# Reading the doubt flag two search parts later on VectorE, in a nearest-neighbour attention kernel

## The reference: what is computed

```python
x = x + _L0_conv_ref(_gn(x), L0_conv_weight, L0_conv_bias)   # 3x3, a weight of its own at each of 3136 points
x = x + _L1_conv_ref(_gn(x), ...)                            # neighbour attention
```

```python
p = p / jnp.maximum(jnp.linalg.norm(p, axis=1, keepdims=True), 1e-12)
dist = _pairwise_distance(p)              # 3136 x 3136 for each image
_, nn_idx = jax.lax.top_k(-dist, K)       # the 16 nearest points of each point
nbr = pts[bidx, nn_idx]
logits = leaky_relu(cat([e, e_n]) @ W_att + b_att, 0.1)
attn = softmax(logits, axis=2)
agg = jnp.sum(nbr * attn, axis=2)
y = cat([pts, agg]) @ W_conv + b_conv     # then batch norm, relu, and + pts
```

## Time and profile before

| | |
|---|---|
| median of three runs | 12411.11 us |
| the profiled execution | 12415.89 us, of which the span from first to last instruction is 12414.2 us |
| mean granted TensorE clock | 0.948 of full speed |
| VectorE busy | 10343.8 us (83% of the span) |
| TensorE busy | 10245.6 us (83%) |
| ScalarE busy | 10206.3 us (82%) |
| GpSimd busy | 3005.3 us (24%) |
| `attend` | from about 1519 us to 12310 us |

### The profile page before, as it was taken

The page is one execution under the profiler, slowest core; times in us unless marked ns, Lnnn a source line. Parts: engine busy times, 40 slices in busy tenths (PEclk is TensorE's granted clock), DMA queues, the critical chain, the costliest instruction groups (busy, mean ns, idle before and its releaser), DMA issues. The chain is left out here.

```text
span 12414.2 us, 345180 instructions
## 1 busy us (share of the span) xinstructions
PE 10245.6 (83%) x125146; PEld 7668.4 (62%) x125146; DVE 10343.8 (83%) x23897; ACT 10206.3 (82%) x11576; POOL 3005.3 (24%) x1648
## 2 busy tenths in 40 slices
PE   2774678888888888888888888888888888878875
PEld 2564356666666666666666666666666666656654
DVE  1000599999999999999999999999999999999997
ACT  2332489999898999989999998898998989979986
POOL 0000022222222222222222222222222222222221
PEclk9897889999999999999999999999999999999998
DMA  9666800000000000000000000000000000000003
GB/s 153 169 167 175 254 9 16 17 16 16 16 16 16 16 16 16 5 16 16 16 17 16 17 16 16 16 17 16 17 16 4 16 16 17 16 15 16 16 4 127
DMA packets 267617, 481.85 MB, mean 39 GB/s; under 512 B 196964, under 2 KB 197348, under 8 KB 248356
## 3 DMA queue, kind: packets, MB, share of 16 engines
q1 hardware_dynamic: 261348, 407.82, 13.9%
q0 software_dynamic: 4608, 51.38, 1.2%
HBM read 353.59 MB, written 105.50 MB: 37 GB/s over the span
## 5 line engine op out<-in xcount | busy, mean ns | idle before, releaser
L871 PE MATMUL psum<-ident_a,masked 128*128 128x128 f32 (+1 forms) x40000 | 5529.8, 286 | 575.0 <-ACT turned_sb L991 485.1
L871 PEld LDWEIGHTS psum<-ident_a,masked 128*128 128x128 f32 (+1 forms) x40000 | 4790.7, 193 | 1807.9 <-issue 1733.2
L820 POOL TENSOR_TENSOR masked<-masked,shares_a 128x784 f32<-128x784 f32 x1600 | 2984.7, 1865 | 7765.8 <-DVE doubts L1068 5058.4
L1062 DVE MAX8 found<-scores 128x8 f32<-128x224 f32 x11200 | 3440.0, 378 | 138.6 <-ACT scores L964 63.8
L991 ACT ACTIVATE turned_sb<-psum 128x512 f32<-128x512 f32 (+1 forms) x5600 | 2948.5, 565 | 251.4 <-PE psum L871 177.3
L964 ACT ACTIVATE scores<-psum 128x1568 f32<-128x1568 f32 x1600 | 2372.8, 1483 | 825.4 <-DVE minus_top L1101 712.8
L1101 DVE CUSTOM_DVE_ANT_0 masked<-masked,scores 128x3136 f32<-128x3136 f32 x800 | 2724.3, 3405 | 0.2 <-DVE scores L1093 0.2
L976 ACT ACTIVATE masked<-masked,minus_top 128x3136 f32<-128x3136 f32 x800 | 2353.9, 2942 | 0.0
L956 ACT ACTIVATE masked<-shares_a,own 128x3136 f32<-128x3136 f32 x800 | 2328.2, 2910 | 1.0
L848 PE MATMUL psum<-points 32*128 32x392 f32 x12800 | 1596.0, 564 | 29.8 <-DMA rows<-table 16.9
L890 PE MATMUL psum<-turned_sb,rows 128*32 128x128 f32 (+1 forms) x40000 | 1524.8, 281 | 0.5 <-ACT inverse_sb L972 0.5
(11 more groups left out here) (134 smaller groups left out, 5368.6 us busy)
## 6 DMA issues: line engine op xcount, KB each, us to landing
w_in<-in_L_conv_weight_dram SPq DMA_DIRECT2D x784, 144.0 KB, 2.8
points<-unit SPq DMA_DIRECT2D x128, 392.0 KB
shares_a<-share SPq DMA_DIRECT2D x32, 1568.0 KB
windows<-xg SPq DMA_DIRECT2D x42, 928.0 KB, 11.5
xg<-padded SPq DMA_DIRECT2D x32, 406.0 KB, 17.1
table<-table_sb SPq DMA_DIRECT2D x32, 404.2 KB
rows<-table SPq DMA_DIRECT2D x32, 396.0 KB
x_in<-in_x_dram POOLq DMA_DIRECT2D x8, 1568.0 KB, 12.6
```

The costliest lines, as they stand in the source:

```text
L820: nc.gpsimd.tensor_tensor(m, m, shares[:, t.half, k * width:(k + 1) * width], ALU.add).then_inc(logits_ready, 1)
L871: last = nc.tensor.matmul(ps[0:width, bank + u * P:bank + (u + 1) * P], masked[:, t.ring, j * P:j * P + width], ident[:], start=True, stop ...
L1062: n = step(nc.vector.max(found[:, t.par, c, :], scores[:, t.par, c * PART:(c + 1) * PART]))
```

## The change

The search of the coming tile's first half is cut in two: parts 1 and 2 are searched before VectorE reads the doubt sum out of PSUM, parts 3 to 7 behind it. The wait for the scores (`gate` on `scores_in`) goes with the first piece.

```diff
-            def search(t, quad):
-                gate(dve, scores_in, t.count(2, quad + 1), dve_passed)
-                for c in range(quad * EARLY, (quad + 1) * EARLY):
+            def search(t, quad, first=0, last=EARLY):
+                if first == 0:
+                    gate(dve, scores_in, t.count(2, quad + 1), dve_passed)
+                for c in range(quad * EARLY + first, quad * EARLY + last):
                     n = step(nc.vector.max(found[:, t.par, c, :], scores[:, t.par, c * PART:(c + 1) * PART]))
                 return n
...
                 if tile(3):
                     invert_total(tile(3))
+                if coming:
+                    search(coming, 0, 0, 2)
                 if here:
                     ask_doubts(here)
                 if coming:
-                    search(coming, 0)
+                    search(coming, 0, 2)
                 if here:
                     settle_doubts(here)
                     bar(here)
```

## The result

The changed kernel takes 12235.88 us (median of 4 runs, 12233.09 to 12238.46) against 12409.29 us before (4 runs). The ratio is 0.9859, with a 95% interval of 0.9845 to 0.9874: 173 us saved. I had forecast 59 us and a range whose lower end was 12295. The direction was right, and the size was off by a factor of three.

A forecast was written before the change was run, and what follows sets the result against it. VectorE's chain was taken to bound the kernel. Wide tiles' 73 us, less 12 (early) and 6 (narrow), plus 7 (irregular), gave 62, rounded to 59 us saved: 12411 - 59 = 12352 us, range 12295 to 12440.

The forecast's parts named there:

- what bounds, and which waits fall: VectorE's chain bounds `attend`; its wait for TensorE's doubt sum falls from 431 to about 140 us.
- the block: L1092 now overlaps GpSimd's second piece by 0.40 us, stands, and ends 0.83 us after it; median about 1.23 us.
- No block: Rival: L1092 runs its 1.02 us whatever GpSimd does; 234 us saved, 12177 us; chance 8%.
- The whole of L1092 behind GpSimd: Rival: L1092's full 1.02 us comes after GpSimd ends; 94 us slower, 12505 us; chance 4%.
- the wide tile's gain of 0.38: 192 tiles with the wide projection: flag's read to L1092's end falls from 3.30 to 2.92 us; 73 us saved.
- the early tile: 576 tiles with a 0.25 us doubt-sum wait: reciprocal to L1092's end goes from 3.55 to 3.57 us; 12 us lost.
- a small operation is followed by MAX8 after a gap of 0.06: On VectorE, this gap plus two MAX8 of 0.296 puts the flag's read 0.65 us after the reciprocal.
- my lower bound for this term: Early tile: the first MAX8 may start without its 0.06 us gap; 576 x 0.06 = 35 us more saved.
- irregular: About 35 tiles with longer doubt-sum waits, beyond the loop's end, gain 0.19 us each; 7 us saved.
- The narrow tile: 32 tiles with the narrow projection: reciprocal to L1092's end goes from 3.38 to 3.57 us; 6 us lost.
- A drain at the flag: Rival: VectorE finishes MAX8 before the flag's read, which comes at 0.80 us; 29 us slower, 12440 us; chance 8%.
- the wide tiles' gain is waited for elsewhere: Rival: ScalarE or TensorE has no room in the tile behind; only 18 us of losses remain, 12429 us; chance 12%.

The follow-up runs named there:

- small piece: GpSimd's second piece cut from 784 to 16 columns: 12123.75 us on the changed kernel, 12409.72 us on the kernel before.
- Three parts: Changed kernel with the flag read behind three MAX8 instead of two: 12350.85 us.
- wait only: Kernel before with only the gate for the scores put ahead of the flag's read, all seven MAX8 staying behind it: 12283.88 us.
- the kernel before once more: The kernel before, unchanged, run again for its TensorE clock: 12405.29 us in a single run.
- one part: Changed kernel with the flag read behind one MAX8 instead of two: 12185.74 us.
- fewer columns: Changed kernel with 1344 instead of 1568 columns left to GpSimd, its second piece 560 wide instead of 784: 12146.54 us.

## Why the prediction was right or wrong

**Right: what bounds, and which waits fall.** VectorE's chain set the time, and the wait for the sum fell to 111.5 us where I had said about 140. It stayed in the wide tiles.

**Right: the block.** The bar ends 0.83 us behind GpSimd's end, as read from the last tile alone. "No block" is refuted by the bar's 1.37 us and by both small pieces. "The whole of L1092 behind GpSimd" is refuted by the same 0.83. The bar's median was 1.37 rather than 1.23, since the bar itself came sooner.

**Right: the wide tile's gain of 0.38, and that it is kept.** From the read's start to the bar's end it is 32.73 + 1.37 - 31.18 = 2.92 us against 3.30. ScalarE and TensorE still idle 0.61 and 0.85 us in the early tile.

**Wrong: the early tile, "before 3.55, now 0.65 + 2.92 = 3.57, a loss of 0.02".** It measured 3.41, a gain of 0.14. The step that failed is "a small operation is followed by MAX8 after a gap of 0.06", and with it the read at 0.65. I took both gaps from before's read of the flag. The read there was a waiting instruction, with a gate (a register operation and a wait) behind it. Where nothing waits, the first MAX8 starts 0.08 us before the reciprocal ends. That is 0.14 us, and my lower bound for this term allowed 0.06. Moving only the gate showed the rest of the mechanism: what lies behind a waiting instruction starts late if a gate of its own has still to be passed.

The gain of 0.14 isn't to be multiplied by 576, though. The interval into a wide tile is TensorE's: its read came 13.63 us after the one before, and 13.38 after, and those 0.25 are only the earlier tile's read having moved from 0.25 to 0.50. So what an early tile gains just ahead of a wide one is waited for there. 13 of the 25 tiles keep it: 13 x 32 x 0.14 = 58 us, where the sum had -12. These are 70 us of the 114 that were missing.

**Wrong: the clock isn't in the sum at all.** I had 0.948 and the tiles with longer waits before me, called them irregular and gave them 7 us. Early tiles with a low stretch cost 62 us over the others before and 14 after, 48 us less. Three parts, wait only and the kernel before once more each show that the term goes with the program; why it does isn't shown.

Together: 59 + 70 + 48 - 7 (the irregular tiles, taken as the same ones) = 170 us, against 173 measured. That the sum comes so near is partly luck, since each term is good to a few us only.

**Small.** The narrow tile lost 0.03 us rather than 0.19, for the same reason as the early one. A drain at the flag didn't show: the read came 0.58 us after the first MAX8, two steps of 0.29. That the wide tiles' gain is waited for elsewhere didn't come true for this change, but a wait for ScalarE, one of the two engines that this rival named, is what stopped one part, the small piece and fewer columns at 12.44 us. The long waits at the loop's end, which I counted as 16 of some 4.4 us, are 14 in the trace before, 60 us in all; since they were taken to gain nothing, the sum doesn't change.

## What to carry to other kernels

A gap behind a waiting instruction may be due to what the queue holds there, not to the engine's own step; before a step is costed by it, look for the same pair of instructions where neither waits. A gate that stands behind a waiting instruction is paid after that wait, even if its semaphore has long come (0.13 us a tile here, most of it the register operation), and putting the gate first can be most of what a larger move gains (118 of 173 us here, the clock's part in both). When a moved instruction releases another engine, count from its new place to the next operation that the other engine can block, and try the neighbouring places: one part was better than two, and shortening the blocker better still.

## What was not expected of the hardware

- A `tensor_scalar` of 128x1568 that starts while GpSimd is in a `tensor_tensor` ends 0.83 us after GpSimd's end, whether it started 0.25, 0.55 or 0.75 us before that end (one, two, three parts). Its own time is 1.02 us, so 0.19 us of it lie beside the block. An overlap of 0.06 us cost nothing (0.89 us for 1344 columns).
- VectorE's MAX8 started 0.08 us before the end of a reciprocal ahead of it, and 0.06 to 0.08 us after the start of a one-element read of PSUM that takes 0.13 to 0.15 us. It was 0.12 us where a semaphore wait and a count stood between, and 0.21 where a register operation did too; in both cases the read itself had waited.
- TensorE's mean granted clock went from 0.948 in the profiled execution (0.950 to 0.953 in the runs beside it) to 0.960 when one gate of VectorE was put ahead of a read, and 27 of the 118 us gained aren't in the usual tile's length.
- VectorE's MAX8 over scores that ScalarE had just copied started 0.14 us after the copy's end wherever that copy came last.
